# TensorE's order in the first attention: scores of step s+2 ahead of the transposes of step s

## The reference, cut to what matters

```python
Q = apply_rope((X @ Wq).reshape(Bs, Ts, H, dh))        # H = 32 heads, dh = 32
K = apply_rope((X @ Wk).reshape(Bs, Ts, Hkv, dh))      # Hkv = 8, so 4 query heads share a key head
V = (X @ Wv).reshape(Bs, Ts, Hkv, dh)
scores = jnp.einsum('bkgtd,bksd->bkgts', Qh, Kh) / jnp.sqrt(jnp.float32(dh))
scores = jnp.where(causal[None, None, None], scores, -jnp.inf)
attn = jax.nn.softmax(scores, axis=-1)
out = jnp.einsum('bkgts,bksd->bkgtd', attn, Vh)
```

## Time and profile before

| what | us |
|---|---|
| median of 3 runs | 5799.51 |
| the profiled execution | 5802.05 |
| its span | 5800.2 |
| first attention, from the first scores (L623) to the last normalise (L764) | 524.3 to 1479.6 |
| PE busy over the span | 3975.3 (69%) |
| DVE busy over the span | 3821.2 (66%) |
| ACT busy over the span | 3315.8 (57%) |

### The profile page before, as it was taken

One profiled execution on the slowest core, in us unless ns is written; L12 is line 12 of the kernel. 1 busy time (PEld: TensorE's weight loads), 2 busy tenths in 40 slices (PEclk: granted clock), 3 DMA queues, 4 the chain that ended last, 5 costly groups with the idle time before them and its releaser, 6 DMA issues. The chain is left out here.

```text
span 5800.2 us, 80523 instructions
## 1 busy us (share of the span) xinstructions
PE 3975.3 (69%) x23480; PEld 2373.9 (41%) x23480; DVE 3821.2 (66%) x10794; ACT 3315.8 (57%) x7698; POOL 289.1 (5%) x213
## 2 busy tenths in 40 slices
PE   6997888888899989814555545555455554554599
PEld 2444555555444444402333323333233332333354
DVE  1663666666233346458888888888888888888443
ACT  1113666666100011168888888888888888888200
POOL 1331000000000023300000000000000000000000
PEclk7998999999999999956777777777777777777799
DMA  3223222212311132310011010110101100010222
GB/s 122 68 68 70 61 56 48 69 47 50 113 44 43 43 101 68 72 30 21 4 24 23 21 23 4 23 23 21 22 5 23 23 21 17 10 23 5 69 66 80
DMA packets 277680, 250.19 MB, mean 43 GB/s; under 512 B 169968, under 2 KB 210048, under 8 KB 277248
## 3 DMA queue, kind: packets, MB, share of 16 engines
q1 hardware_dynamic: 276704, 245.60, 16.2%
q0 software_dynamic: 544, 0.07, 0.0%
HBM read 168.03 MB, written 77.59 MB: 42 GB/s over the span
## 5 line engine op out<-in xcount | busy, mean ns | idle before, releaser
L1013 ACT ACTIVATE a_sign<-a_x,a_state 128x256 fp8e4<-128x256 f32 (+6 forms) x2240 | 1833.7, 820 | 393.6 <-DVE a_state L1134 254.0
L922 PE MATMUL a_ps_s<-a_k,a_q 128*128 128x512 bf16 (+3 forms) x1536 | 479.5, 454 | 749.6 <-DVE a_x L1241 709.4
L950 PE MATMUL a_ps_o<-a_probT,a_v 128*32 128x128 f32 x4608 | 649.2, 289 | 461.8 <-ACT a_probT L983 457.1
L950 PEld LDWEIGHTS a_ps_o<-a_probT,a_v 128*32 128x32 f32 x4608 | 483.6, 115 | 597.3 <-ACT a_probT L983 548.9
L322 PE MATMUL p_ps_qkv<-p_w,p_hT 128*128 128x512 f32 x1536 | 676.6, 597 | 3.3 <-ACT p_hT L360 2.3
L701 ACT ACTIVATE a_prob<-a_ps_s,a_shift 128x640 f32<-128x640 f32 (+7 forms) x512 | 379.9, 742 | 349.0 <-DVE a_shift L743 304.0
L922 PEld LDWEIGHTS a_ps_s<-a_k,a_q 128*128 128x128 bf16 x1536 | 153.8, 123 | 986.6 <-DVE a_x L1241 809.6
L641 PE MATMUL a_ps_t<-a_ident,a_prob 128*128 128x128 f32 x2304 | 369.3, 286 | 164.8 <-ACT a_prob L701 100.9
L743 DVE TENSOR_REDUCE a_shift<-a_ps_s 128x1 f32<-128x640 f32 (+7 forms) x512 | 384.3, 753 | 111.2 <-PE a_ps_s L626 105.2
L322 PEld LDWEIGHTS p_ps_qkv<-p_w,p_hT 128*128 128x128 f32 x1536 | 289.1, 191 | 348.0 <-issue 344.9
L1145 DVE TENSOR_SCALAR_CACHE_REDUCE a_above<-a_x,a_state 128x256 bf16<-128x256 f32 (+3 forms) x448 | 391.8, 875 | 47.3 <-issue 38.2
(11 more groups left out here) (200 smaller groups left out, 5292.3 us busy)
## 6 DMA issues: line engine op xcount, KB each, us to landing
a_q<-qk SPq DMA_DIRECT2D x256, 256.0 KB, 4.9
qk<-p_qkT SPq DMA_DIRECT2D x32, 960.0 KB, 6.2
p_h<-h SPq DMA_DIRECT2D x32, 512.0 KB, 7.0
a_k<-qk SPq DMA_DIRECT2D x256, 64.0 KB, 5.1
m_o<-o SPq DMA_DIRECT2D x32, 512.0 KB, 5.4
m_h<-h SPq DMA_DIRECT2D x32, 512.0 KB, 5.5
p_w<-in_wqkv SPq DMA_DIRECT2D x16, 768.0 KB, 12.5
h<-tok_h SPq DMA_DIRECT2D x16, 512.0 KB, 2.6
```

The source lines that it names most:

```text
L922: nc.tensor.matmul(ps_s[:, n % 2, a:a + w], q[:, y, head, i * P:(i + 1) * P], k[:, y, a:a + w], start=(y == 0), stop=False, skip_group_che ...
L950: mm = nc.tensor.matmul(ps_o[strip:strip + DH, c:c + P], v[:, b * DH:(b + 1) * DH], probT[:, n % 2, b * P:(b + 1) * P], start=(b == 0), st ...
L1013: ins = nc.scalar.activation(sign[:, off(i):off(i) + w], x[:, par, at:at + w], ACT.Sign, scale=-1.0, saturate=False, bias=state[:, par, 0, ...
```

## The change

On PE, within each step, the scores of step s+2 are issued ahead of the transposes of step s. Nothing else is changed: the same instructions with the same semaphores and the same values waited for, and the lists of DVE, ACT, POOL and SP are as they were. `values` still comes last in its step, so it now stands behind `turn(s)`.

```diff
@@ -666,9 +666,9 @@
                         scores(0)
                         scores(1)
                     for s in range(STEPS):
-                        turn(s)
                         if s + 2 < STEPS or not last:
                             scores(s + 2)
+                        turn(s)
                         if s % SPU == 1 and not (first and s < SPU):
                             values(s // SPU - 1)
                     if last:
```

## The result

The changed kernel takes **5828.93 us**, the median of 5 runs (5828.03 to 5832.36), against 5799.51 for the kernel before in the same session: ratio 1.0054, 95% interval [1.0039, 1.0068]. It is slower, as forecast, but by 29 us and not by 78.

A forecast was written before the change was run, and what follows sets the result against it. A chain through the engines was taken to bound the stage, with no engine full. Legs summed to +5.01 us a group, +80 over 16 groups, -2 at edges: 5878 us; 5840 to 5925 for 8 times in 10.

The forecast's parts named there:

- leg C: From the end of the values to the sixth exponential of a unit: walked at 16.91 us a group.
- leg B: From the second wide exponential to the end of the values, which come sooner: walked at 20.71 us a group.
- No difference: Rival: PE's total decides, or both orders meet the same later wait; 5800 us, 5%.
- Score-first pays: Rival: scores begun in PE's gap ahead of its transposes feed the slow maximum sooner; 5774 us, 5%.
- Units (5,2) and (4,3): Units named by wide and narrow block counts; these short ones lose most, +1.42 and +2.04 us.
- The clock: Rival: PE's granted clock falls more often as its work thins out; 5948 us, 7%.
- Durations: Linear fits by block count for exponential, maximum, copy, transposes and scores, plus values, normalise and hand-overs, read from profile rows.
- leg A: From a unit's eighth exponential to the second wide exponential, with DVE's copy ahead of the maximum: walked at 14.90 us a group.
- Leg D: From the sixth to the eighth exponential, all narrow: 11.06 us a group; for (4,3) 3.65 new, 2.81 old order.
- S(2): Scores of 2 blocks on PE, from weight load to the next transposes: 0.40 us.
- S(8): Scores of 8 blocks on PE, from weight load to the next work: 1.03 us.
- The loop's edge: Five edges where PE waits for instructions and the clock falls: -0.3 us each, between -1.1 and +0.8; -2 in sum.

The follow-up runs named there:

- max_first_new: Changed kernel with DVE also taking the maximum of step s+2 ahead of its copy of step s: 5712.5 us, ratio 0.9851 to the kernel before.
- short copies: DVE's copies of turned chunks cut to one column, in the kernel before and the changed kernel: first-attention stage 911.9 us in the old order, 902.7 in the new.

## Why the prediction was wrong in size

**What held.** The mechanism and its place: DVE's copy between scores and maximum, in wide and odd narrow steps and not in the even ones. In the wide steps what it costs in leg C is nearly paid for by leg B; the net cost is that of the odd narrow steps. The signs: leg B (the values sooner) is the leg that gains, and each of the others loses. Units (5,2) and (4,3) pay most (+0.58 and +1.07 us by the earlier trace rows and their counterpart). "No difference" is out. "Score-first pays" was right about PE's gaps, and failed where the prediction said, at DVE: the copy still came last. With DVE's list moved too (max_first_new, another kernel) the order on PE does pay, and the scores on PE wait 90.3 us for the exponential from 600 to 1400 us, against 138.3 in the changed kernel. There the trace agrees with what the prediction cited from "Perfetto Trace Analysis" of the Trainium skill, section "Optimization Strategy". The clock is no cause of the loss: from 600 to 1400 us it was 0.99 in the mean in both kernels, and unit (6,1) of the changed kernel had it at 1.00, the 2.4 GHz level, with PE busy 12.14 of 14.73 us (windows view of that unit, columns as in the earlier trace rows):

```profile
842.93:857.66 14.73, 12.14 (x146) 8.68 (x143) 9.20 (x16) 8.88 (x23) 0.40 (x1) 1.00 0.89 201
```

**What failed: the terms of "Durations".** Each leg was walked along the right path with terms too long, so that +5.01 us a group came out where 1.69 was measured. The prediction named as a sign of being wrong that the first attention's end moves less than 40 us; it moved 25.4. The group shown above, leg by leg (marks: the eighth, second and sixth exponentials, and the first matmul or transpose that PE starts behind the values, at 829.68 in the earlier trace rows and 837.30 above):

| leg | before | walked | measured | too much |
|---|---|---|---|---|
| A | 13.09 | 14.90 | 13.84 | 1.06 |
| B | 21.88 | 20.71 | 20.33 | 0.38 |
| C | 14.78 | 16.91 | 16.13 | 0.78 |
| D | 8.82 | 11.06 | 9.96 | 1.10 |
| sum | 58.57 | 63.58 | 60.26 | 3.32 |

Against before, A lost 0.75, B gained 1.55, C lost 1.35 and D lost 1.14. Since the loss is a small difference of large sums, 5% of error in the walk made two thirds of the forecast. Leg D of (4,3), walked at 3.65 and measured at 3.37, shows the terms (timeline of the changed kernel):

```profile
884.31 0.69 ACT L701 ACTIVATE a_prob<-a_ps_s,a_shift 128x512 f32<-128x512 f32 x1 [0.49 <-DVE a_shift L743]
...
885.14 0.11 PEld L623 LDWEIGHTS a_ps_s<-a_k,a_q 128*128 128x128 bf16 x2 [0.66 <-ACT a_prob L701]
...
885.58 0.42 PEld L641 LDWEIGHTS a_ps_t<-a_ident,a_prob 128*128 128x128 f32 x4
...
886.28 0.69 DVE L753 COPY a_probT<-a_ps_t 128x512 f32<-128x512 f32 x1 [1.28 <-PE a_ps_t L641]
...
886.89 1.81 DVE L743 TENSOR_REDUCE a_shift<-a_ps_s 128x1 f32<-128x512 f32 x2
```

- *Scores, from load to the next transposes*: 0.44 us, not 0.61. The row used for S(2) had its load start behind transposes still running, and S(8) was put together from the landing of scores behind transposes. On an idle PE the stretch is shorter: 0.88 for 8 blocks (833.02 to 833.90), not 1.03. Where PE was still turning, the changed kernel's stretch for 8 blocks is 0.97. Excess 0.15 to 0.17.
- *Copy to the next instruction of DVE*: the maximum starts 0.61 us behind the copy's start, before its 0.69 have passed. The walk had 0.69 + 0.03. Excess 0.11. The kernel before shows it as well, in a row that the prediction left unread: its copy of the earlier trace rows ends at 824.97, and in the timeline the next work starts sooner:

```profile
824.88 0.19 DVE L758 RECIPROCAL a_inv<-a_total 128x8 f32<-128x8 f32 x1
```

- *Exponential to PE*: 0.14, not 0.21 (885.00 to 885.14). Excess 0.07.
- *Transposes until the copy*: 0.70, as walked. *Maximum to exponential*, with the maximum: 0.79, not 0.72, the one term of this leg that was too short. The hand-over of 0.04 from one row is the rarer one: 132 exponentials of the changed kernel follow their maximum by 0.03 to 0.04 us, and 300 by 0.11 to 0.13.

Sum of the excess: 0.17 + 0.11 + 0.07 - 0.07 = 0.28, the difference of this leg. With 0.15 for wide scores the same four terms give 0.26 a unit in leg A, 1.04 of its 1.06.

"VectorE: DVE Perf Modes" of the Trainium skill, section "The DRAIN you can't avoid", says that a next operation waits until the engine's pipeline is empty, and that one that is not held starts earlier. It gives no figure for the second case. Both traces have the next instruction ahead of the copy's recorded end (-0.09 and -0.08 us).

**The check that misled.** Leg D in the old order came out at 2.81 against 2.93 measured, which the prediction took as a test. That leg has no scores on an idle PE and no copy ahead of its maximum, so it tested none of the terms that the new order adds. It was also short by 0.12 where the new leg was long by 0.28. The range allowed 1.4 us a group for such errors; they came to 3.3, because the same few terms recur in every leg, nearly all with one sign.

**The loop's edge.** Beside the medians of their units, the five edges cost 11.8 us together before and 9.4 after. That is -2.4, forecast at -2 in sum, but it came so by luck. The forecast kept the clock's fall at every edge, and most of the difference is the clock: in the changed kernel's trace it fell behind only two of the five edges (2.59 and 2.74 us) and stayed at 1.00 behind three (1.21, 1.35 and 1.54), while it fell behind all five of the kernel before (2.20 to 2.62). Edges with a fall are thus no shorter than before, and the 0.3 us an edge that the walk took off for them is not seen.

## What to carry to other kernels

An order of issue on one engine pays only as far as the consumer's own list fits it: find the next instruction that needs the result, and read what stands ahead of it in that engine's queue. Swap by step class before swapping everything; here two steps in eight, swapped alone, cost as much as all eight, two others brought a gain, and moving the consumer as well turned 29 us of loss into 87 of gain. And in a sum that is the small difference of two long chains, take hand-overs from start to start, in a row where the engine is in the state that the new order will have.

## What the runs showed of the hardware

DVE starts its next instruction 0.08 to 0.09 us before the recorded end of a copy out of PSUM, behind all 384 such copies of the changed kernel. A copy of one column takes 0.15 to 0.16 us (short copies), one of 512 columns 0.69. The scores of 8 blocks, from their load to the next transposes, take 0.88 us on a PE that was idle, against the 1.03 put together from scores behind transposes. At the loop's edge the changed kernel's PE waited too, 2.20 us at the second edge, for nothing that the profile shows, and the granted clock behind it was 0.68, part of the stretch at the 1.2 GHz level, much as before. Behind the fourth edge, after a wait of 2.63 us, it stayed at 1.00, the 2.4 GHz level. So a longer wait did not bring the fall, and what decides it stays open (timeline of the second edge, then windows view of both):

```profile
892.26 1.86 PE L623 MATMUL a_ps_s<-a_k,a_q 128*128 128x512 bf16 x4 [2.20 <-issue]
```

```profile
892.20:897.60 5.40, 5.34 (x26) 3.59 (x26) 1.57 (x3) 1.62 (x3) 0.40 (x1) 0.68 0.02 5
1138.80:1144.00 5.20, 5.20 (x82) 4.08 (x86) 3.13 (x5) 2.23 (x6) 0.40 (x1) 1.00 0.02 6
```
